# Zero blocks and scatters among the attention's batches of a graph network: three zero blocks per batch in place of two, scatters from batch 21 in place of 32

## The reference

```python
k_e, q_e, v_e = k[src], q[dst], v[src]
a = (_typed_rel(k_e, rel_att, etype) * q_e).sum(-1) * rel_pri.T[etype] / jnp.sqrt(D)
ex = jnp.exp(a - amax[dst])
attn = ex / jnp.maximum(segment_sum(ex, dst)[dst], 1e-09)
h = segment_sum(_typed_rel(v_e, rel_msg, etype) * attn[:, :, None], dst)
```

```python
agg = segment_sum((x @ W)[src] * norm[:, None], dst)   # norm = dinv[src] * ew * dinv[dst]
```

## Time and profile before

| | |
|---|---|
| time, median of 3 runs | 4404.68 us (4403.91 to 4405.47) |
| the profiled execution's own time | 4402.57 us |
| its span, first to last instruction | 4400.2 us |
| PE / PEld busy | 3591.3 us (82%) / 2515.2 us (57%) |
| DVE / ACT / POOL busy | 2413.3 / 1140.0 / 2612.3 us |
| bytes moved by DMA | 1026.64 MB |
| the attention's turns of logits (L894) | 621.9 to 1941.3 us |
| scatters L498, first and last start | 1318.8 and 2161.0 us |

### The profile page before, as it was taken

How to read it: one execution, slowest core, us unless ns; L and a number is a source line. 1 busy time by engine, 2 the same in 40 slices (tenths; PEclk the granted TensorE clock), 3 DMA queues, 4 the chain that set the end, 5 groups by cost and what they waited for, 6 DMA issues and landing times.

```text
span 4400.2 us, 57750 instructions
## 1 busy us (share of the span) xinstructions
PE 3591.3 (82%) x17006; PEld 2515.2 (57%) x17006; DVE 2413.3 (55%) x8286; ACT 1140.0 (26%) x2513; POOL 2612.3 (59%) x2737
## 2 busy tenths in 40 slices
PE   3677758888888777665499999979999969999993
PEld 3565557778777666662355555545555545555552
DVE  3334447777777656569245444445544454554446
ACT  1111147887778565542200000000000000000001
POOL 0000047666667777778577777737677755767772
PEclk8788878898888777878799999989999979999996
DMA  6787867777783333320387888758788858778871
GB/s 189 226 292 291 291 229 280 280 284 270 270 289 99 87 94 91 88 79 1 108 334 292 299 300 300 285 193 299 286 298 299 300 187 301 293 289 299 299 290 49
DMA packets 273376, 1026.64 MB, mean 233 GB/s; under 512 B 66086, under 2 KB 126021, under 8 KB 234160
## 3 DMA queue, kind: packets, MB, share of 16 engines
q1 hardware_dynamic: 157760, 714.07, 43.6%
q0 software_dynamic: 103792, 266.94, 18.4%
q10 hardware_dynamic: 11520, 41.95, 3.3%
HBM read 797.16 MB, written 225.58 MB: 232 GB/s over the span
## 4 chain that ended last, share of the span: by engine, by line
PE 62%; POOL 17%; DVE 9%; issue 7%; DMA 2%; SPq 2%; ACT 0%; POOLq 0%; DVEq 0%; ACTq 0%
PE bank L1003 36%; POOL arena L518 8%; PE bank L975 8%; POOL a_tab L498 7%; PE bank L843 3%; PE bank L858 3%; PE bank L861 3%; PE bank L792 2%; DVE arena L1052 2%; PE bank L803 2%; PE bank L789 2%; POOL stage L543 1%; PE bank L778 1%; PE bank L1008 1%; DVE arena L1150 1%
## 5 line engine op out<-in xcount | busy, mean ns | idle before, releaser
L543 POOL DMA_INDIRECT stage<-h_tab,earr x1536 | 1453.0, 946 | 715.8 <-issue 362.1
L1003 PE MATMUL bank<-arena,xr 128*128 128x512 f32 (+1 forms) x3822 | 1695.0, 590 | 44.5 <-DMA arena<-a_tab 38.6
L1003 PEld LDWEIGHTS bank<-arena,xr 128*128 128x128 f32 x3822 | 698.4, 191 | 758.7 <-issue 742.4
L518 POOL DMA_INDIRECT arena<-kv_tab,idxr x832 | 801.0, 963 | 351.6 <-issue 241.8
L1508 DVE TENSOR_TENSOR sums<-sums,bank 128x128 f32 x1536 | 432.9, 282 | 815.4 <-PE bank L975 809.2
L1479 DVE TENSOR_SCALAR oh<-iota_j,earr 128x128 f32<-128x128 f32 x1536 | 585.4, 384 | 87.7 <-DVE sums L1499 45.3
L698 ACT ACTIVATE rs<-mv,epsc 128x49 f32<-128x49 f32 (+1 forms) x6 | 1.9, 316 | 2114.5 <-DVE mv L1542 2012.8
L975 PEld LDWEIGHTS bank<-oh,stage 128*128 128x128 f32 x3072 | 409.0, 196 | 233.8 <-issue 187.8
L843 PE MATMUL bank<-xr,arena 128*128 x3328 | 435.2, 290 | 77.3 <-DVE arena L1204 50.3
L975 PE MATMUL bank<-oh,stage 128*128 128x128 f32 x3072 | 420.8, 282 | 51.1 <-DMA stage<-h_tab,earr 41.6
L843 PEld LDWEIGHTS bank<-xr,arena 128*128 128x128 f32 x3328 | 414.9, 205 | 82.2 <-issue 81.0
(11 more groups left out here) (216 smaller groups left out, 3065.2 us busy)
## 6 DMA issues: line engine op xcount, KB each, us to landing
arena<-a_tab SPq DMA_DIRECT2D x273, 1792.0 KB
a_tab<-stage SPq DMA_DIRECT2D x60, 1792.0 KB
a_tab<-sums POOLq DMA_DIRECT2D x31, 1792.0 KB, 11.9
kv_tab<-stage SPq DMA_DIRECT2D x48, 768.0 KB, 8.2
arena<-rel_d SPq DMA_DIRECT2D x52, 512.0 KB, 15.4
stage<-h_tab,earr POOLq DMA_INDIRECT x1536
arena<-key_d ACTq DMA_DIRECT2D x40, 512.0 KB, 5.0
arena<-in_edge_weight ACTq DMA_DIRECT2D x40, 512.0 KB, 8.4
```

Source lines behind the costliest of these rows:

```text
L518: G.indirect_dma_start(kv[b % 3][:, t, :], None, kv_tab, bass.IndirectOffsetOnAxis(idxr[:, b % 3, t:t + 1], 0))\
L543: G.indirect_dma_start(gring[:, (q % NG) * GRP + s, :], None, h_tab[l], bass.IndirectOffsetOnAxis(src_i[:, t:t + 1], 0)).then_inc(row_land ...
L1003: mm = M.matmul(o_[:, 0:cw], xr[:, n, :], abuf[B % NBUF][:, n % KB, 0:cw], start=n == 0, stop=n == NT - 1)
```

## The change

ZB, the number of zero blocks per batch, goes from 2 to 3, so that the 60 blocks go out with batches 1 to 20. SB goes from 32 to 21. The 160 scatters among the gathers get their places from a list: four per batch (one per group) in batches 21 to 42, and eight (two per group) in the last nine, 43 to 51. The 48 after the last gather and the 112 after the bias add stay.

```diff
-SB = 32
-SPB = 8
+SB = 21
 SY = 48
-ZB = 2
+ZB = 3
...
+            places = [b for b in range(SB, NB) for _ in range(2 if b >= NB - (160 // NG - (NB - SB)) else 1)]
+            slots = [(b, g) for b in places for g in range(NG)]
+
             def gather(b):
...
                 for g in range(NG):
-                    if b >= SB:
-                        for k in range(SPB // NG):
-                            scatter(SPB * (b - SB) + k * NG + g)
+                    for t, at_ in enumerate(slots):
+                        if at_ == (b, g):
+                            scatter(t)
                     if b >= 3:
...
-            for t in range(SPB * (NB - SB), min(T1, SPB * (NB - SB) + SY)):
+            for t in range(len(slots), len(slots) + SY):
                 scatter(t)
...
-            for t in range(SPB * (NB - SB) + SY, T1):
+            for t in range(len(slots) + SY, T1):
                 scatter(t)
```

## The result

The changed kernel takes 4433.48 us (median of 4 runs, 4430.1 to 4435.56) against 4404.3 for the kernel before, measured beside it: a ratio of 1.0067, interval 1.0051 to 1.0082. That is 29 us slower, where 4436 us were forecast. Its profiled execution has a span of 4432.8 us, 32.6 more than before.

What follows compares the result with a forecast made beforehand. POOL was taken to bound the kernel from the first scatter on, the PE chain before it. Terms of -31.6 + 23.7 + 39.6 = +31.7 us against the median 4404.68 gave 4436 us, with 8 in 10 from 4397 to 4458.

Steps and rivals of the forecast that it cites:

- The saving in the scatters: POOL, batches 21 to 51: four scatters a batch in 22 batches, eight in nine, 840.0 us against 871.6; saves 31.6 us.
- The wait at the first scatter: POOL before batch 21's scatters: idles for the last zero blocks, starting at turn 19 + 17.1; loses 23.7 us (20 to 30).
- The third zero block: SP's queue, batches 2 to 19: it delays the rel_d load behind it, stalling PE 2.2 us a batch; loses 39.6 us.
- The price of a block: SP's queue: each zero block ahead of the rel_d load makes that load land 6.2 us later.
- the forecast's own loop: Load issued from turn b-2, needed behind turn b-1: lateness of 4.4 us, past 1.8 slack, halves to 2.2 us a batch.
- third rival: PE's clock: new stalls bring 16 matmuls at 1.2 GHz into each batch, +15 us on top, 4451 us; chance 0.2.
- the hidden block: Rival at the rel_d load: third block's delay stays within the 1.8 us slack, no stall, sum -8 us; chance 0.15.
- the half stall: Rival at the rel_d load: stall near 0.9 us a batch, block at 3.6 us, sum +8, 4413 us; chance 0.1.
- the signs: Expected in the changed profile: rel_d landing about 22 us after issue, 25 to 26 us batches, first scatter near 1126.

Runs made afterwards that it cites:

- the fastest kernel: Changed kernel with zero blocks behind the rel_d load from batch 3 on, batch 1's in their old place, scatters from batch 22: 4393.95 us against 4404.52, ratio 0.9976.

## Why the prediction was right, and where it was right by luck

**The saving in the scatters** was 31.6 us as forecast, 32.3 as measured. A batch with four scatters was put at 25.6 and is 25.6 in the mean of its pairs; the stretch is 839.25 us for a forecast of 840.0.

**The wait at the first scatter** was put at 23.7 us and is 25.9. POOL idled in front of it as described, and the run with scatters from batch 22 shows that this time is lost. What was off is the landing of the last zero blocks: the first scatter was put at turn 19 + 17.1, and it came at + 19.3. The packets of three blocks without gathers beside them took 14.8 us (1112.4 to 1127.2), those of the last two blocks with gathers 12.6 (1305.1 to 1317.7). By their bytes, 5.5 and 5.8 MB, the forecast had taken the two for equal.

**The third zero block** was put at 39.6 us ahead of turn 19, and turn 19 is 40.0 later. The cause is the named one: the idle times are at L845 behind L896, ACT waits for rel_d, and the load ahead of the zero blocks takes most of it away. But the terms inside are not those of the forecast, and that they add up to 40 is in part luck:

- The price of a block was put at 6.2 us. The landing moved by 3.5 us (19.7 against 16.2), and three issues took 2.79 us where two took 1.21, 1.6 more: 5.1 us. In the stretch of the kernel before that matches (675 to 1086 us) the load landed 15.8 us after its issue, which makes it 5.5. With the forecast's own loop that is a stall of 1.65 to 1.85 us a batch ((5.1 - 1.8) / 2 and (5.5 - 1.8) / 2), 30 to 33 us in all and not 40.
- The stall is not the same in each batch. A stall behind one turn gives the next load more time, so only the sum of two stalls is fixed; in the changed kernel's trace they came as 2.0 to 3.4 us in one batch and 0 to 0.3 in the next. The mean length fits all the same.
- The forecast counted from a batch of 23.66 us, but three of the 18 before took only 22.1 to 22.9, and the mean of all is 23.45. That is 0.2 us a batch more to lose, 4 us.
- The rest came behind the stall. After an idle 2.03 us PE's 32 matmuls took 5.43 us and not 3.74, at a granted clock of 0.69. That is the third rival's mechanism, which had chance 0.2 and was meant to come on top of the full stall. The forecast's argument that 2.2 us of idle time are too short for it was wrong; behind 2.46 us the clock stayed at 1.00, so the length of the idle time alone doesn't tell. It is worth about 4 us here, and 35 us are lost without it. These 4 and the 4 of the shorter mean made up for the smaller price of the block; the errors cancelled.

The rivals: the hidden block falls by the run with three blocks alone (+47 us, not 0), the half stall by the length of the batches (25.63 us, 2.2 over the mean before, where it had 0.9). The loss in that run is larger than the 42 us expected, by 5 us, and it is larger than the change's own, as the sum of the three terms says it must be.

Of the signs, the load landed 19.7 us after its issue and not 22, and the batches were in the mean as long as said but uneven. The others held: the first scatter at 1128.3 (1126 forecast), the last gather at 1967.6 (1966), the GCN layers of the same length within 2.4 us.

## What to carry to other kernels

When a large background transfer is put on a queue, ask what small load stands behind it there, from which event that load is issued and what needs it: two blocks per batch cost nothing here, and most of what the third one cost came from its place ahead of a 0.5 MB load. Move the small load ahead before adding to the large one. And when the first user of a background job is moved earlier, move the job's end by as much: one batch of distance in place of two left the bottleneck engine idle for 32 us, and a second batch of distance took 17.5 us off the time.

## What was not expected of the hardware

Register loads by an engine's sequencer (TENSOR_LOAD of four words of SBUF) took 0.34 us while the DMA engines had a light time and up to 1.4 us while they were full, in the same place of the program. In the kernel before, PE's own register loads show the same: a median of 0.65 us and up to 1.23 in the batches with zero blocks (710 to 1060 us), 0.33 in those without (1420 to 1890 us). With the load ahead of the zero blocks a batch stayed at 23.9 to 24.0 us, 0.5 above the old one; DVE's longer register loads are seen there, in the fastest kernel too, but that they are all of it was not tested.

Three DMA issues of the same kind on SP took 2.79 us, more than twice the 1.21 of two. And in some sessions every kernel of this study took 5542 to 5564 us, on a chip too that gave 4404.9 in another session: DVE's, ACT's and POOL's instructions had the same durations (0.42, 0.71 and 0.97 us for L1299, L632 and L518, 900 to 1060 us), and there were long pauses between PE's, at a granted clock of 0.73 in the batch shown.
